# Linear recurrence: DVE scans one place in four, PE forms step ends and outputs from tables of powers

## What is computed

```python
lam = exp(-exp(nu_log) + 1j * exp(theta_log))         # 256 complex numbers
B_norm = gamma_log[:, None] * (B_re + 1j * B_im)      # 256 x 128
Bu = einsum('btd,hd->bth', u, B_norm)
h_t = h_{t-1} * lam + Bu_t                            # along the 166 places of a sequence
y = real(einsum('tbh,oh->bto', h, C_re + 1j * C_im)) + einsum('btd,od->bto', u, D)
```

## Time and profile before

| | us |
|---|---|
| median of 3 runs (lowest to highest) | 2369.14 (2367.48 to 2370.04) |
| the profiled execution | 2365.66 |
| its span, first to last instruction | 2363.9 |
| tokens and tables, to the barrier | 0 to 32.3 |
| norm n1 | 32.3 to 54.0 |
| recurrence | 54.0 to 293.9 |
| next norm begins | 294.9 |

### The profile page before, as it was taken

One profiled execution on the slowest core, in us unless ns is written; L12 is line 12 of the kernel. 1 busy time (PEld: TensorE's weight loads), 2 busy tenths in 40 slices (PEclk: granted clock), 3 DMA queues, 4 the chain that ended last, 5 costly groups with the idle time before them and its releaser, 6 DMA issues.

```text
span 2363.9 us, 36022 instructions
## 1 busy us (share of the span) xinstructions
PE 1949.7 (82%) x9514; PEld 1065.9 (45%) x9514; DVE 1920.2 (81%) x2945; ACT 1340.0 (57%) x1979; POOL 1525.3 (65%) x1165
## 2 busy tenths in 40 slices
PE   7677661066799679658999999999999999999998
PEld 5444340044556578533444444444444444444443
DVE  5999862067355787498999999999999999999998
ACT  3000031054134245357887888888878888888887
POOL 1344306700589550436888888888888888888887
PEclk9888875599799699758999999999999999999999
DMA  4400201151133220313433345444454444344443
GB/s 98 137 18 18 80 1 43 51 93 34 45 103 124 89 89 1 128 50 108 140 137 135 132 141 210 138 139 139 141 203 137 139 139 141 138 136 150 152 144 112
DMA packets 122750, 257.21 MB, mean 109 GB/s; under 512 B 40212, under 2 KB 56244, under 8 KB 121012
## 3 DMA queue, kind: packets, MB, share of 16 engines
q1 hardware_dynamic: 119988, 250.78, 33.0%
q0 software_dynamic: 2688, 5.44, 0.7%
HBM read 219.13 MB, written 29.59 MB: 105 GB/s over the span
## 4 chain that ended last, share of the span: by engine, by line
PE 45%; DVE 7%; issue 3%; ACT 2%; DMA 1%; POOL 0%; DVEq 0%; ACTq 0%; SPq 0%; POOLq 0%
PE bank L2018 24%; PE bank L2032 20%; DVE hc L1950 3%; ACT bank L1870 2%; DMA m_share<-expert_shares 1%; DVE hc L1954 1%; DVE bank L1947 1%; DVE m_work L1932 1%; PE bank L2039 0%; DVE m_best L1929 0%; DVE h L1958 0%; DVE m_work L1923 0%; DVE m_ut L638 0%; DVE m_best L1922 0%; PE bank L630 0%
## 5 line engine op out<-in xcount | busy, mean ns | idle before, releaser
L1870 ACT ACTIVATE bank<-bank,m_b 128x896 f32<-128x896 f32 x768 | 753.3, 981 | 202.9 <-PE bank L2018 202.8
L1827 POOL TENSOR_TENSOR hc<-hc 128x896 f16<-128x896 f32 x384 | 725.4, 1889 | 31.9
L2032 PE MATMUL bank<-hc,weights 128*128 128x448 f16 x3072 | 706.9, 353 | 8.3 <-DVE h L1958 7.1
L1825 POOL TENSOR_SCALAR hc<-hc 128x896 f16<-128x896 f32 x384 | 359.8, 937 | 173.1 <-PE bank L2032 115.4
L1950 DVE TENSOR_TENSOR hc<-bank,m_share 128x896 f32<-128x896 f32 x384 | 418.9, 1091 | 53.8 <-ACT bank L1870 15.7
L2018 PE MATMUL bank<-m_u_first,weights 128*128 (+1 forms) x1536 | 422.8, 357 | 28.2 <-DVE hc L1950 11.9
L2032 PEld LDWEIGHTS bank<-hc,weights 128*128 128x128 f16 x3072 | 298.7, 98 | 297.2 <-issue 15.4
L1947 DVE TENSOR_TENSOR bank<-bank,m_share 128x896 f32<-128x896 f32 x384 | 418.5, 1090 | 11.0 <-ACT bank L1870 6.2
L1954 DVE TENSOR_TENSOR hc<-bank,hc 128x896 f16<-128x896 f32 x384 | 415.1, 1081 | 5.4 <-ACT hc L1873 5.4
L2018 PE MATMUL bank<-m_u_second,weights 128*128 (+1 forms) x1536 | 418.4, 354 | 0.0
L1873 ACT ACTIVATE hc<-bank 128x896 f16<-128x896 f32 x384 | 351.7, 916 | 38.4 <-DVE bank L1947 25.9
(11 more groups left out here) (300 smaller groups left out, 2489.7 us busy)
## 6 DMA issues: line engine op xcount, KB each, us to landing
m_share<-expert_shares SPq DMA_DIRECT2D x384, 448.0 KB, 3.6
ew_raw<-e_w_dram SPq DMA_DIRECT2D x32, 512.0 KB, 4.5
expert_factors<-ew_made SPq DMA_DIRECT2D x24, 512.0 KB, 3.0
weights<-expert_factors SPq DMA_DIRECT2D x12, 1024.0 KB, 9.4
expert_slots<-lru_zeros SPq DMA_DIRECT2D x1, 7296.0 KB, 28.2
lru_wst<-w_dram SPq DMA_DIRECT2D x16, 256.0 KB, 2.7
weights<-w_dram SPq DMA_DIRECT2D x1, 4096.0 KB, 12.4
xs<-x_dram SPq DMA_DIRECT2D x4, 996.0 KB, 12.3
```

The lines of the kernel that those rows point to most:

```text
L1825: g.tensor_scalar(h_first[:, x, 1], hs[:, x], 1.0 - SHARE, 1.0, ALU.mult, ALU.mult).then_inc(first_of[1], 1)
L1827: g.tensor_tensor(h_second[:, x, 1], hs[:, x], h_first[:, x, 1], ALU.subtract).then_inc(second_of[1], 1)
L1870: sc.activation(bank, bank, ACT.Gelu, bias=b1[:, bass.ds(grp * GE + e, 1), c]).then_inc(gelu[c], 1)
L2032: last = t.matmul(banks_y[:, q], k.weights[:, grp % 2, 2 + m, at], hh[:, e % 2, c, q * HW:(q + 1) * HW], start=(grp > 0 and e == 0 and c = ...
```

## The change

A sequence's 166 places are taken in steps of four (`STEP`; `LC` = 42 steps, the last one short). If the state is known at the end of every step, the output at place i of a step follows from the state at the end of the step before, times C lambda^(i+1), and from the i + 1 inputs of the step itself, times real 128x128 matrices (`lags`). And what a step adds to its end is a sum of its four inputs, each times B lambda^(3-i) (`w_in`). So PE does more and DVE scans 42 columns per sequence instead of 166. The work is grouped by eight sequences (`GB`; 336 columns `GC`, four groups of four chunks).

- `constants_and_tokens`: angles for 45 times (`TIMES`) instead of 166; powers of |lambda|; `factor`; `w_out` (C times powers, twelve products of 512 columns on DVE); four transposes of B on PE between the token chunks (`pe_turn_inputs`), scaled by gamma on DVE (`b_turned`); four tables `on_diag` on POOL. The weights' DMAs are issued between the second and third part of the tokens. DVE starts only when POOL's constants are made (`MADE`).
- `recurrence`: PE first forms `w_in` (8 matmuls of 512 columns) and `lags` (4, and one of 128), which ACT copies to SBUF. `ut` holds three groups, ordered by place in the step. `step_ends` has 16 matmuls per group, `output` 5 to 8 per place. DVE runs `normed` (now two instructions per chunk, written with a stride), `state_part`, and `add`, which adds a bank straight into `h` with a stride of four columns. POOL no longer adds; it makes diagonals and splits, four splits ahead of each of the last three pairs of diagonals.

```diff
+    def pool_diagonals(self, pool, ident):
+        pool.wait_ge(self.factors_made, 1)
...
+            dve.wait_ge(made, MADE)
             tables.dve_tables(dve)
...
-            def work(c, j):
-                state(c, 0)
-                if exists(c + 1):
-                    normed(c + 1, 1 - j)
-                state(c, 1)
...
+            def normed(c):
+                v.tensor_tensor(out[:, :, 0:L // STEP], x[:, :, 0:whole].rearrange("p b (s i) -> p b s i", i=STEP),
+                                r[:, :, 0:whole].rearrange("p b (s i) -> p b s i", i=STEP), ALU.mult)
+                v.tensor_tensor(out[:, :, LC - 1, 0:L - whole], x[:, :, whole:], r[:, :, whole:], ALU.mult).then_inc(u_ready, 1)
+            def state_part(g, p):
+                dve.wait_ge(ends, m + 1)
+                v.tensor_tensor(by_step(va[:]), pair, tab(cos, p), ALU.mult).then_inc(turned, 1)
+                v.tensor_tensor(by_step(vb[:]), pair, tab(sin, p), ALU.mult).then_inc(turned, 1)
...
+                for q, op in enumerate((ALU.subtract, ALU.add)):
+                    v.tensor_tensor(state_of[:, g % 2, p, q, :, 1:], xc[:, q].rearrange("p (b s) -> p b s", b=GB),
+                                    xsn[:, 1 - q].rearrange("p (b s) -> p b s", b=GB), op).then_inc(state, 1)
+            def add(g, i):
+                dve.wait_ge(y_ready, n + 1)
+                v.tensor_tensor(h, h, k.bank[:, 6 + i % 2, 0:GC].rearrange("p (b s) -> p b s", b=GB)[:, :, 0:steps],
+                                ALU.add).then_inc(y_added, 1)
+            for g in range(NGR):
+                if g + 1 < NGR:
+                    state_part(g + 1, 0)
+                add(g, 0)
+                add(g, 1)
+                if g + 2 < NGR:
+                    normed((g + 2) * PERG)
+                    normed((g + 2) * PERG + 1)
+                if g + 1 < NGR:
+                    state_part(g + 1, 1)
+                add(g, 2)
...
+            def step_ends(g):
+                pe.wait_ge(u_ready, PERG * (g + 1))
+                for p in range(2):
+                    if g:
+                        pe.wait_ge(turned, 2 * (2 * (g - 1) + p) + 2)
...
+                        for i in range(STEP):
+                            last = t.matmul(k.bank[:, 2 + 2 * p + q, 0:GC], w_in[:, p, q, STEP - 1 - i], ut[:, g % UB, i],
+                                            start=(i == 0), stop=(i == STEP - 1))
```

More of the change, by code:

```diff
@@ L432, in recurrence @@
         block = ctx.enter_context(nc.Block())
-        def exists(c):
-            return not isinstance(c, int) or 0 <= c < NC
-        def chunks(eng, work):
-            for c in range(2):
-                work(c, c)
-            with eng.Fori(1, NC // 2 - 1) as i:
-                for j in range(2):
-                    work(2 * i + j, j)
-            for c in range(NC - 2, NC):
-                work(c, c % 2)
         w0 = k.weights[:, 0].rearrange("p a b -> p (a b)")
@@ L492, in work @@
-                g.tensor_tensor(k.h[:, chunk(c)], k.h[:, chunk(c)], ysb[:, j, :], ALU.add).then_inc(y_added, 1)
+            for c in range(2):
+                diagonal(c)
             g.memset(zeros[:], 0.0).then_inc(zeros_made, 1)
-            for j in range(2):
-                diagonal(j, j)
-            chunks(pool, work)
+            for c in range(2, 2 * PERG + 2):
+                diagonal(c)
+            done = 0
+            for c in range(2 * PERG + 2, NC, 2):
+                for n in range(done, done + 4):
+                    split(n)
+                done += 4
+                diagonal(c)
+                diagonal(c + 1)
@@ L499, in _ @@
+            for n in range(done, NC):
+                split(n)
         @block.scalar
         def _(act):
-            act.sem_inc(y_copied, 2)
-            act.sem_inc(y_added, 2)
-            with act.Fori(0, NC // 2) as i:
-                for j in range(2):
-                    act.wait_ge(y_ready, 2 * i + j + 1)
-                    act.wait_ge(y_added, 2 * i + j + 1)
-                    nc.scalar.activation(ysb[:, j, :], k.bank[:, 6 + j, 0:CH], ACT.Copy).then_inc(y_copied, 1)
+            sc = nc.scalar
@@ L511, in _ @@
             v = nc.vector
[L512 to L529 removed]
+            cos, sin = tables.ang[:, 2], tables.ang[:, 1]
@@ new lines, in in_tables, with lag_tables @@
+            def in_tables(p):
+                for q, factors in enumerate((((0, 0), (2, 1)), ((0, 1), (1, 0)))):
+                    for n, (part, m) in enumerate(factors):
+                        last = t.matmul(k.bank[:, 2 + 2 * p + q, :], b_turned[:, p, part],
+                                        on_diag[:, m, p].rearrange("p i d -> p (i d)"), start=(n == 0), stop=(n == 1))
+                last.then_inc(in_product, 1)
+            def lag_tables():
+                products = [(p, part) for p in range(2) for part in range(2)]
+                for n, (p, part) in enumerate(products):
+                    last = t.matmul(k.bank[:, 6, :], b_turned[:, p, part], w_out[:, 0:STEP, p, part], start=(n == 0), stop=(n == 3))
+                    if n == 0:
+                        t.matmul(k.bank[:, 6, 0:128], k.ident[:], tables.w_d[:], start=False, stop=False)
+                last.then_inc(lag_product, 1)
@@ new lines, in output @@
+            def output(g, i):
+                n = STEP * g + i
+                if n >= 2:
+                    pe.wait_ge(y_added, n - 1)
+                bank = k.bank[:, 6 + i % 2, 0:GC]
+                for j in range(i + 1):
+                    t.matmul(bank, lags[:, j], ut[:, g % UB, i - j], start=(j == 0), stop=False)
+                for p in range(2):
+                    if i == 0:
+                        pe.wait_ge(state, 2 * (2 * g + p) + 2)
+                    for q in range(2):
+                        last = t.matmul(bank, w_out[:, i + 1, p, q], state_of[:, g % 2, p, q, :, 0:LC], start=False,
+                                        stop=(p == 1 and q == 1))
+                last.then_inc(y_ready, 1)
@@ new lines, in _ @@
+            for c in range(2):
+                spread_rstd(c)
+            pe.wait_ge(tables.done, 1)
+            pe.wait_ge(tables.diag_made, 4)
+            for p in range(2):
+                in_tables(p)
+                spread_rstd(2 + p)
+            lag_tables()
+            step_ends(0)
+            for c in range(PERG, 2 * PERG):
+                spread_rstd(c)
+            pe.wait_ge(lag_ready, 1)
+            step_ends(1)
+            for g in range(NGR):
+                if g + 2 < NGR:
+                    spread_rstd((g + 2) * PERG)
+                    spread_rstd((g + 2) * PERG + 1)
+                for i in range(STEP):
+                    output(g, i)
+                    if g + 2 < NGR and i == 2:
+                        spread_rstd((g + 2) * PERG + 2)
+                        spread_rstd((g + 2) * PERG + 3)
+                if g + 2 < NGR:
+                    step_ends(g + 2)
```

282 lines of the change are left out of this document (169 added, 113 removed).

## The result

The changed kernel takes 2282.44 us in the median of 4 runs (2276.05 to 2292.63); the kernel before took 2368.31 beside it. The ratio is 0.9642, with an interval of 0.9605 to 0.9678: 3.6% faster. The forecast was 2290, its range 2265 to 2310. The profiled execution (2281.96) has a span of 2280.2 us against 2363.9. Behind the new functions all lines have moved by 142: L2018 is now L2160.

The account below looks back on a forecast made before the run. DVE was taken to bound the recurrence (239.9 us). 2365.66 - 239.9 + 153.5 (new recurrence) + 7.4 (tables) = 2286.7 us for the profiled execution, which lies 3.5 under the median, so 2290; range 2265 to 2310.

Parts of the forecast that it names:

- The bound: Old recurrence: DVE sets the stage, busy 147.80 of 150 us; the stage lasts 239.9 us.
- The state parts: Recurrence: DVE's state parts take 6.7 us alone and 10.6 with POOL always busy.
- The factor 1.59: Old recurrence: DVE's eight instructions take 9.14 us beside a busy POOL, 1.59 times their 5.74 with POOL idle.
- Rival A: Recurrence: the shared port costs little, parts take 6.7 to 8 us, total 2267 to 2278; chance 0.22.
- B: Recurrence: DVE waits out a whole POOL instruction per SBUF instruction, 13.8 us per part, total 2313; chance 0.12.
- The order of events: Recurrence: the sequence of PE, DVE and POOL steps counted from the stage's start, ending at 153.5 us.
- PE's idling before group 2: Recurrence: PE idles over 6 us before group 2's step ends, then runs the first eight matmuls mostly at low clock.
- The strided instructions: Recurrence: strided DVE instructions take 0.85 us, 0.95 with the small tail, bounds 0.5 and 1.2.
- PE's tables: Start of the recurrence: 13 matmuls for the tables, 10.4 us, done with two spreads between at 16.8 us.
- The table stage: End of the first block: DVE's longer chain of table products adds 7.4 us, bounds +4 and +11.
- What the first 294 us lose or gain comes straight off the total: Whole kernel: later stages are untouched behind barriers of all engines, so early gains or losses pass fully into the total.
- Rival C: Recurrence: PE's clock stays low after idling, total 2373; chance 0.01 slower, 0.01 same, 0.05 partly lost (2300 to 2320).

Follow-up runs that it names:

- e1: Changed kernel without POOL's sixteen weight splits in the recurrence, split weights set to zero: 2256.69 us, ratio 0.9564 to the kernel before.
- e8: Changed kernel with the cast and scaling of each split on ACT instead of POOL: 2280.76 us, ratio 0.9631 to the kernel before.
- e4: Changed kernel with POOL's four diagonal tables made during norm n1 instead of the first block's end: 2275.32 us, ratio 0.9621 to the kernel before.
- e3: Changed kernel with DVE's output-table products moved into the recurrence and PE's lag tables made later: 2262.87 us, ratio 0.9571 to the kernel before.
- e5: Changed kernel with sixteen unread PE matmuls filling PE's idling before norm n1: 2281.18 us, ratio 0.9642 to the kernel before.
- e6: Changed kernel with e2's order, e3's late tables and four early POOL splits, weight loads ahead of the slots' zeros: 2264.97 us, ratio 0.9572 to the kernel before.
- changed_again: The changed kernel run once more, unaltered, beside the kernel before on the same chip: 2280.98 us, ratio 0.9672.
- e2: Changed kernel with all four chunks normalised before the second state part, spreads, diagonals and splits moved to match: 2272.90 us, ratio 0.9610 to the kernel before.
- e7: As e6, but with two early splits instead of four: 2258.82 us, ratio 0.9544 to the kernel before.
- e9: Changed kernel with e2's order, e3's late tables and e8's split steps on ACT, no early splits: 2250.00 us, ratio 0.9505 to the kernel before.

## Why the prediction was right, point by point

**The bound.** That DVE sets the old recurrence, and that taking its work away shortens the stage by what the order of events gives, held: 88.5 us against 86.4.

**The state parts.** 6.7 alone and 10.6 beside POOL were forecast. Two took 6.8, six 10.53 to 11.38. The factor 1.59 from the earlier trace rows came out as 1.6 (10.91 / 6.76), on other sizes and new instructions, and e1 shows that POOL's splits are its cause. Rival A (parts under 8) and B (13.8) both fell. B's mechanism is there for single instructions. The Trainium skill, page "SBUF — State Buffer", section "SBUF: two separate sides", says that whichever of DVE and GpSimd comes first holds the shared pair for its whole instruction. The rows of e8 agree, for both directions. What made B too dear is that it charged each of a part's eight SBUF instructions with a whole one of POOL's, 0.89 us: in the second part (103.57 to 114.48, 10.91 us for 6.76) the eight lost 4.15 us together, 0.52 each. That DVE gets in during POOL's pauses of 0.2 us would explain it; no run tests that.

**The order of events.** Counted from 64.65, against the forecast: eighth chunk normalised 28.5 (30.1), both first parts 49.8 (51.3), part (1, 0) 60.8 (61.9), last chunk of group 2 76.7 (78.9), group 2's states begin 83.0 (85.2), last chunk of group 3 109.8 (112.7), group 3's states 116.6 (119.0), end 151.4 (153.5). The first split at 31.0 (30.7), the last at 113 (117). Every step stands in its place, up to 2.9 us early. PE's idling before group 2 was put at over 6 us and was 3.00. The last chunk came 2.2 us sooner, and PE's work before it, put at 3.9 + 1.1 + 4.5 = 9.5 us, took 12.1: the prediction charged the low clock behind PE's wait for the step ends, and not behind the wait of 6.36 us for an addition that its own order of events has before it. The same six instructions behind that wait, and one group later without one:

```profile
126.22 3.73 PE L714 MATMUL bank<-lru_ut,lru_lags 128*128 128x336 f32 x6 [6.36 <-DVE h L635]
...
159.47 1.96 PE L714 MATMUL bank<-lru_ut,lru_lags 128*128 128x336 f32 x6
```

This miss cost the sum nothing, since PE was done before the last chunk all the same; DVE's wait of 5.77 and 6.29, forecast as 6.3, is what counts.

**Mis-sized terms.** The strided instructions: a normalised chunk takes 0.71 and its tail 0.16, 0.61 from start to start, where 0.95 was taken; the addition 0.75, or 0.66 from start to start, for 0.85. L829, the nearest row, was too dear a bound for a stride of four elements. That gave some 2.4 us away in the first 80. PE's tables, done 15.6 us into the stage for 16.8, gave another 1.2. Against it, the parts beside POOL were longer than forecast, 10.95 in the mean for 10.6, which took back 1.4 in the same stretch: together the 2.2 us by which the last chunk of group 2 came early.

**The table stage.** +8.5 for +7.4. e4 splits it: without POOL beside it DVE ends at 36.62, forecast 37.3; POOL's four tables cost 3.7, forecast 2. The factor of 1.59 was too low here, where nearly all of DVE's instructions read two operands from SBUF: 0.69 became 1.42 to 1.55, and DVE lost almost the whole of the 4.0 us that POOL needs alone.

**What was left out.** "What the first 294 us lose or gain comes straight off the total" was not wholly right: norm n1 lost 2.2 us, since PE idles 9.65 us before it (e3 and e5 take the idling away, and its first matmuls have their 2.47 us again). Rival C looked for the clock inside the recurrence, where it was 0.91, and not at the stage behind a longer first block. And the untouched rest came out 5.8 us lower in the first pair of profiles, 3.9 in the second. Without both, the forecast's sum would have been 2286.7 + 1.1 (tables) - 2.1 (recurrence) = 2285.7; n1 adds 2.2 and the rest takes 5.8: 2282.1, which is the profiled execution's 2282.0. Of the 7.6 us between forecast and median, 3.6 are n1 and the rest together, 1.0 is the terms, and 3.0 come from adding 3.5 for the distance of before's profiled execution to its median, which is 0.5 in the changed kernel. So the forecast's mechanism is borne out, but that the sum for the profiled execution came within 5 us is in part luck: the tables' 1.1 and n1's 2.2 stand against the recurrence's 2.1, and the rest's 5.8 belong to no term.

## What to carry to other kernels

Price an instruction of DVE beside a busy POOL by rows in which the two already meet, and price the place, not the mean: products in a chain of SBUF operands took twice their time, a part with PSUM readers 1.6 times. When a serial chain on one engine grows in front of a barrier, look at how long PE idles there, and charge the next stage for the clock; and charge every wait of PE in the order of events, not only the one that is looked at. And when two improvements use the same gap (e6: late tables and early splits), the second can cost more than it brings; count what shares the port there first.

## What the runs showed of the hardware

PE's cold start is not one number. Behind the 9.65 us of idling, norm n1 took 23.9 and 24.3 us in three profiles of five (changed, changed_again, e1) and 39.3 in the two others (e2, e8), at a granted clock of 0.50 throughout, with PE busy 36.7 of the 39.3 us. Without that idling (e3, e5, e6, e7, e9), or with 6.33 us of it (e4), n1 took 21.7 to 23.8 in every profile. Single executions fit in part: with the long idling the times of the changed kernel are 2276.05 to 2298.63, with e3 2261.02 to 2263.89 and with e4 2274.21 to 2277.72. But e5, e6, e7 and e9, without the idling, lie within 9.6 to 11.6 us, so n1 is not all that varies. That those executions without a profile that took 15 us longer had the same n1 is likely and not shown. The Trainium skill, page "TensorE: Matmul & The Clock Gate", section "What's actually happening", says that the number of slow matmuls differs from run to run and advises against fitting to it, the penalty being under 1% of a span. The rows agree on the size: 15.4 us are 0.7% of the span, though nearly a fifth of what this change was worth. A low level that lasts through a whole norm with PE nearly always busy, as in e2 and e8, is more than the slow start of which that section tells.

DVE cleared 4032 columns in 3.42 us (L638), as estimated by columns from a small one. ACT's cast and scaling of 512 columns, 0.63 us, are as fast as POOL's (0.61 and 0.62) and cost DVE nothing in the rows of e8 that stand beside them.
